# A perceiver layer's cross-attention: values of four batches weighed in one visit, sixteen probability buffers, context loads in pairs

## The chip, the cores and the metric

One core of a Trainium2 chip (trn2). The metric is the device time of the kernel in microseconds; a single execution is also recorded by the profiler. TensorE (PE) multiplies matrices, VectorE (DVE) and ScalarE (ACT) work on tiles in SBUF and PSUM, GpSimd (POOL) on tiles in SBUF, and SyncE (SP) issues the loads and stores. Every engine runs its own list of instructions in order and waits on semaphores that the others raise.

## What is computed

One layer over 128 batches of 32 tokens of 128 features: cross-attention to a context of 257 rows, then self-attention, then a mixture of experts. The change lies in the cross-attention, whose core in the reference is (16 heads of 8 features):

```
def _L0_xattn_ref(queries, keys, values, mask):
    q = queries.reshape(B, L, H, -1); k = keys.reshape(B, S, H, -1); v = values.reshape(B, S, H, -1)
    scores = jnp.einsum('blhe,bshe->bhls', q, k)
    A = jax.nn.softmax(scale * scores, axis=-1)
    A = A * mask
    out = jnp.einsum('bhls,bshd->blhd', A, v)
    ...
x = x + _L0_xattn_ref(_layernorm(x, axis=-1), ctx_1024, ctx_1024, fside_SxS2_0)
```

Here L is 32, S is 257, and keys and values are the same context. All of it is in float32.

## The kernel before

The 128 batches go in 16 tiles of eight (TB = 8). A tile has two halves of four batches (HB = 4) and 16 steps; the half of a step is its number divided by 8. A step takes two groups of heads, so two steps make a batch. The first and the last tile are written out, the 14 between run in a loop on every engine. In the text, step s means the step of that number in a half (0 to 7) or, above 7, in a tile (8 to 15).

*A step.* TensorE computes the scores of step s into one of two PSUM buffers SC (`scores`, L425). VectorE takes the row maxima (`maxima`, L613, instruction neg_max<-SC), ScalarE the exponentials and their sums (`exponentials`, L551, E<-SC). Two steps later TensorE turns these probabilities into a PSUM buffer ETP (`turn_probs`, L439, ETP<-ident,E), and VectorE multiplies them with the mask into a buffer of Et (`keep_probs`, L621). The scores of step s+2 wait for the exponentials of step s, which free the SC buffer. Each of the float32 score and value products stands as two instructions in the trace.

*A visit.* `weigh_values` (L450, AV<-Et,V) multiplies a batch's values, four groups of 32 columns, with its probabilities into the PSUM tile AV. TensorE's `lagging` calls it for two batches at a time, behind the scores and the turn of probabilities of steps 3, 7, 11 and 15. Et has eight buffers, one for each step of a half.

*Beside the steps.* TensorE's `steps` puts further work at fixed steps: after the scores of steps 0 and 8 `turn_queries` turns the normalised tokens xn (L404); in steps 2, 10, 6 and 14 `turn_keys` turns two batches of the context V into keys (L394), before the turn of probabilities in steps 2 and 10, behind it in steps 6 and 14; in steps 5 and 13 `turn_out` gathers the outputs (L462). All three go through one PSUM tile, MISC. The keys of steps 6 and 14 wait there until `own_outputs` has taken the outputs out (o_n). ScalarE copies keys (`keep_keys`, L533) and queries (`keep_queries`, L541) out of MISC; the scores of step 8 and of the next tile's step 0 wait for the keys turned in steps 6 and 14.

*VectorE's order* in a half: the maxima of a step, then the probabilities of two steps before. In between, at step 3, `invert`; at step 4, the token statistics (`norm_stats`, L580) ahead of the maxima and, behind them, the outputs out of AV (`keep_sums`, L640), `norm_mean`, the probabilities, `norm_var` and `last_probs`; at step 5, behind the probabilities, `own_outputs` (L652, O_n); at step 7, behind the probabilities, in the first half of a tile the transposition of O_n (`turn_tile`, L661), and then `normalise` (L600), which writes xn for the transpose that TensorE does in the next step.

*The loads* are on SyncE's queue, whose order is written out in its `steps`: x for the next tile, last context rows, and V (`load_ctx`, two batches, 256 KB) each behind a wait for the engine that frees its buffer. V has one buffer for each batch of a tile; the load of pair k waits until the visit that read the pair before is over (av_ps counts weighed batches).

Of the kernel before, what the change touches and what calls it, by code (L numbers as in the profile page):

```python
# [14 lines left out]
B, L, D = 128, 32, 128  # L15
# [7 lines left out]
P = 128  # L23
NQ, HQ = 4, 4
# [10 lines left out]
def perceiver_layer(nc, x, ctx, fmask, Wq, bq, Wk, bk, Wv, bv, Wo, bo, gate_w, w1, b1, w2, b2, ln_g, ln_b, out):  # L35
    with ExitStack() as es:
# [67 lines left out]
        with ExitStack() as s1:  # L104
            def sb1(name, shape, dt=F32):
                return s1.enter_context(nc.sbuf_tensor(name, shape, dt))
# [27 lines left out]
            E = sb1("E", [P, 2, HB * NQ, S])  # L134
            den = sb1("den", [P, 2, HB * NQ])
            rden = sb1("rden", [P, HB * NQ])
            Et = sb1("Et", [P, HSTEPS, 2, KT, HQ * L])
            O_m = sb1("O_m", [P, HB, HQ * L])
            O_n = sb1("O_n", [P, DK, TB * NQ])
            O_t = sb1("O_t", [P, DK, L])  # L140
# [52 lines left out]
            @block.sync  # L193
            def _(sp):
                def load_residual(q):

                    for b in range(TB):
                        sp.dma_start(X[32 * q + NQ * b:32 * q + NQ * b + NQ, :, :],
                                     x.rearrange("(t b) (g q e) c -> q b g t (e c)", t=T, g=NQ, q=HQ)[q, b]).then_inc(xperm_in, 16)

                def steps(t, fresh):

                    sp.wait_ge(xn_sb, 2 * t + 1)
                    sp.nop(nofuse=True)
                    load_x(sp, t + 1, 0)
                    sp.wait_ge(qt_ps, 2 * t + 1)
                    sp.nop(nofuse=True)
                    load_last(sp, t + 1, 0)
                    if not fresh:
                        sp.wait_ge(av_ps, TB * t)  # L210
                        sp.nop(nofuse=True)
                        load_ctx(sp, t, 3)
                        sp.wait_ge(o_last, 2 * t)
                        sp.nop(nofuse=True)
                        load_all(sp, t, 1)
                    if fresh:
                        for q in range(HQ // 2):
                            load_residual(q)
                    sp.wait_ge(av_ps, TB * t + 2)
                    sp.nop(nofuse=True)  # L220
                    load_ctx(sp, t + 1, 0)
                    sp.wait_ge(xn_sb, 2 * t + 2)
                    sp.nop(nofuse=True)
                    load_x(sp, t + 1, 1)
                    sp.wait_ge(qt_ps, 2 * t + 2)
                    sp.nop(nofuse=True)
                    load_last(sp, t + 1, 1)
                    sp.wait_ge(av_ps, TB * t + 4)
                    sp.nop(nofuse=True)
                    load_ctx(sp, t + 1, 1)  # L230
                    sp.wait_ge(o_last, 2 * t + 1)
                    sp.nop(nofuse=True)
                    load_all(sp, t + 1, 0)
                    if fresh:
                        for q in range(HQ // 2, HQ):
                            load_residual(q)
                    sp.wait_ge(av_ps, TB * t + 6)
                    sp.nop(nofuse=True)
                    load_ctx(sp, t + 1, 2)

                sp.dma_start(fm[:, :], fmask).then_inc(setup_in, 16)
                load_x(sp, 0, 0)
                load_last(sp, 0, 0)
                load_ctx(sp, 0, 0)
                for n, src in zip("qkvo", (Wq, Wk, Wv, Wo)):
                    sp.dma_start(W[n][:, :], src).then_inc(w2_in, 16)
                for i, src in enumerate((bq, bk, bv)):
                    sp.dma_start(brow[i:i + 1, :], src.unsqueeze(0)).then_inc(w2_in, 16)
                sp.dma_start(bo_row[:, :], bo.unsqueeze(0)).then_inc(w2_in, 16)
                sp.dma_start(b1_rows[:, :], b1.rearrange("e (a f) -> (e a) f", a=FH)).then_inc(b1_in, 16)  # L250
                load_x(sp, 0, 1)
                load_ctx(sp, 0, 1)
                load_last(sp, 0, 1)
                load_ctx(sp, 0, 2)
                load_ctx(sp, 0, 3)
                load_all(sp, 0, 0)
                load_all(sp, 0, 1)
                steps(0, True)
                with sp.Fori(1, T - 1) as t:
                    steps(t, False)  # L260
                sp.wait_ge(av_ps, TB * (T - 1))
                load_ctx(sp, T - 1, 3)
                sp.wait_ge(o_last, 2 * (T - 1))
                load_all(sp, T - 1, 1)

                sp.dma_start(W1[:, :, :], w1.rearrange("e c f -> c e f")).then_inc(w3_in, 16)
                sp.dma_start(G[:, :], gate_w).then_inc(w3_in, 16)
                for a in range(FH):
                    sp.dma_start(W2[:, :, a, :], w2[:, a * P:(a + 1) * P, :].rearrange("e f d -> f e d")).then_inc(w3_in, 16)
                sp.dma_start(b2r[:, :, :].rearrange("p e d -> p (e d)"),  # L270
                             b2.rearrange("e d -> (e d)").unsqueeze(0).to_broadcast([P, NE * D])).then_inc(w3_in, 16)
                sp.dma_start(gr[:, :, :].rearrange("p e d -> p (e d)"),
                             ln_g.rearrange("e d -> (e d)").unsqueeze(0).to_broadcast([P, NE * D])).then_inc(w3_in, 16)
                sp.dma_start(b_rows[:, :], ln_b).then_inc(w3_in, 16)
# [98 lines left out]
            def _(pe):  # L373
# [68 lines left out]
                def weigh_values(t, j, first=False):  # L442

                    h = j // HB
                    pe.wait_ge(et_sb, STEPS * t + 2 * j + 2)
                    if j % HB == 0 and not first:
                        pe.wait_ge(o_m, 2 * t + h)
                    for k in range(KT):
                        for g in range(NQ):
                            i = pe.matmul(AV[32 * g:32 * g + 32, j % HB, :], V[:, j, k, 32 * g:32 * g + 32],  # L450
                                          Et[:, 2 * (j % HB) + g // 2, g % 2, k, :],
                                          start=(j % HB == 0 and k == 0), stop=(j % HB == HB - 1 and k == KT - 1),
                                          skip_group_check=True)
                    i.then_inc(av_ps, 1)
# [11 lines left out]
                def back(t, s, lag):  # L466

                    return (t, s - lag) if s >= lag else (t - 1, s + STEPS - lag)

                def lagging(t, s):  # L470

                    fresh = isinstance(t, int) and t == 0
                    if not (fresh and s < 2):
                        tt, ss = back(t, s, 2)
                        turn_probs(tt, ss, first=fresh and s < 4)
                    if s % 4 == 3 and not (fresh and s < HSTEPS - 1):
                        tt, ss = back(t, s, 2 + 5)
                        weigh_values(tt, ss // 2, first=fresh and s < HSTEPS)
                        weigh_values(tt, ss // 2 + 1)
                    if s % HSTEPS == 5 and not (fresh and s < HSTEPS):  # L480
                        tt, ss = back(t, s, HSTEPS)
                        turn_out(tt, ss // HSTEPS)
# [39 lines left out]
                run_tiles(steps, pe)  # L522
                turn_probs(T - 1, STEPS - 2)
                turn_probs(T - 1, STEPS - 1)
                weigh_values(T - 1, TB - 2)
                weigh_values(T - 1, TB - 1)
                turn_out(T - 1, 1, final=True)

            @block.scalar
# [47 lines left out]
            def _(dve):  # L577
# [37 lines left out]
                def keep_probs(t, s, first=False):  # L615

                    n = STEPS * t + s
                    dve.wait_ge(et_ps, n + 1)
                    if not first:
                        dve.wait_ge(av_ps, TB * t + s // 2 - 3)  # L620
                    dve.tensor_tensor(Et[:, s % HSTEPS, :, :, :].rearrange("p u k c -> p (u k c)"), ETP[s % 2][:, :],  # L621
                                      mask_T[:, :, :, :].rearrange("p u k c -> p (u k c)"), ALU.mult).then_inc(et_sb, 1)

                def invert(t, h):
# [41 lines left out]
                def steps(t, fresh, final):  # L666
                    for s in range(STEPS):
# [6 lines left out]
                            norm_mean(t + 1, s // HSTEPS)  # L674
                        if not (fresh and s < 2):
                            tt, ss = back(t, s, 2)
                            keep_probs(tt, ss, first=fresh and s < HSTEPS + 2)
# [1028 lines left out]
```

## Time and profile before

| | us |
|---|---|
| median of 3 runs | 1048.88 (1048.84 to 1049.33) |
| the profiled execution | 1050.45 |
| its span in the profile | 1048.7 |
| busy: TensorE matmul / weight load | 927.9 / 815.4 |
| busy: VectorE / ScalarE / GpSimd | 840.0 / 648.9 / 606.9 |

The cross-attention is the first half of the span: its first visit starts at 36.4 us and its last ends near 525 us; self-attention and the experts follow. The mean granted clock of TensorE is 0.965 of 2.4 GHz over the span. The rows shown further below are of three kinds: sums over a stretch (windows), sums over a line, and single entries of the timeline, each with its start, its duration, the engine, the line and the tile that is written and read; a bracket at the end gives idle time before it and what ended that. A duration may overlap the next one's start on the same engine, since the engines are pipelined; the distance between two starts is what one of them cost.

### The profile page before, as it was taken

To read this page: it belongs to the slowest core of one execution; us is meant where nothing else is said; L and a number is where in the kernel's file an instruction comes from. 1 tells how busy PE (TensorE), PEld (TensorE's weight loads), DVE (VectorE), ACT (ScalarE), POOL (GpSimd) and SP (SyncE) were. 2 spreads that over 40 slices of the span, in tenths; PEclk is the share of its full clock that TensorE was granted. 3 is DMA by queue.
4 is the path that set the end of the run, shared out by engine and by line. 5 is a ranking of instruction groups with operands and counts; after the bars stand their busy time and mean duration, and the time that the engine had idled before them with its cause. 6 is when DMAs were issued, how large, how long until landed. Compare 5 with 4: busy or idle time off the path is not lost. (4 is left out here: it accounts for less than half of the span.)

```text
span 1048.7 us, 25999 instructions
## 1 busy us (share of the span) xinstructions
PE 927.9 (88%) x7666; PEld 815.4 (78%) x7666; DVE 840.0 (80%) x2152; ACT 648.9 (62%) x2006; POOL 606.9 (58%) x531
## 2 busy tenths in 40 slices
PE   3959999999999999999948888878899888888983
PEld 2848888888888888888848888778788787878872
DVE  5747787878788787878758887886499999999995
ACT  2626566656666566666536666666477777767674
POOL 4335555655555564556344444443477777877786
PEclk9979999999999999999969998999999999999997
DMA  4021212212221212221400000000000000000000
GB/s 119 25 74 56 58 50 65 55 47 60 55 65 43 65 55 52 56 65 54 142 1 1 0 0 0 0 0 1 1 2 10 5 10 5 10 5 6 9 5 16
DMA packets 48676, 35.34 MB, mean 34 GB/s; under 512 B 3660, under 2 KB 48392, under 8 KB 48648
## 3 DMA queue, kind: packets, MB, share of 16 engines
q1 hardware_dynamic: 48648, 35.00, 12.2%
q8 instruction: 14, 0.23, 0.1%
q14 instruction: 14, 0.11, 0.0%
HBM read 32.88 MB, written 2.10 MB: 33 GB/s over the span
## 5 line engine op out<-in xcount | busy, mean ns | idle before, releaser
L551 ACT ACTIVATE E<-SC,neg_max 128x257 f32<-128x257 f32 x512 | 238.4, 471 | 161.2 <-DVE neg_max L613 161.1
L425 PE MATMUL SC<-Kt,Qbd 128*128 128x257 f32 x1024 | 279.6, 396 | 1.0 <-ACT E L551 0.8
L613 DVE TENSOR_REDUCE neg_max<-SC 128x2 f32<-128x514 f32 x256 | 177.0, 691 | 86.6 <-PE SC L425 75.2
L425 PEld LDWEIGHTS SC<-Kt,Qbd 128*128 128x128 f32 x1024 | 176.9, 193 | 31.4 <-issue 14.1
L301 POOL TENSOR_TENSOR Qbd<-Qt,head_scaled 128x2048 f32<-128x2048 f32 (+2 forms) x33 | 145.1, 4398 | 80.0 <-ACT Qt L541 80.0
L621 DVE TENSOR_TENSOR Et<-ETP,mask_T 128x512 f32<-128x512 f32 x256 | 174.0, 680 | 15.0 <-PE ETP L439 14.9
L439 PE MATMUL ETP<-ident,E 128*128 128x128 f32 x1024 | 156.1, 275 | 0.0
L1371 PE MATMUL PO<-W,hid 128*128 128x128 f32 x1024 | 138.2, 278 | 18.8 <-ACT hid L1412 18.7
L1371 PEld LDWEIGHTS PO<-W,hid 128*128 128x128 f32 x1024 | 131.4, 192 | 29.0 <-issue 21.5
L1436 ACT ACTIVATE Y<-Z,zb,zs 128x128 f32<-128x128 f32 x256 | 111.0, 485 | 60.1 <-DVE zb L1591 60.1
L439 PEld LDWEIGHTS ETP<-ident,E 128*128 128x128 f32 x1024 | 125.3, 142 | 20.5 <-issue 0.4
L1360 PE MATMUL PH<-xT,W 128*128 128x256 f32 x512 | 135.1, 387 | 0.5 <-ACT xT L1404 0.5
L1412 ACT ACTIVATE hid<-PH,b1c 128x256 f32<-128x256 f32 x256 | 105.5, 463 | 19.3 <-PE PH L1360 17.8
L551 ACT ACTIVATION_READ_ACCUMULATOR E<-SC,neg_max 128x1 f32 x512 | 101.1, 198 | 0.0
L308 POOL TENSOR_TENSOR xrs<-xvar,neg_half 128x1 f32<-128x1 f32 x32 | 17.6, 549 | 134.8 <-DVE xvar L593 134.8
L1360 PEld LDWEIGHTS PH<-xT,W 128*128 128x128 f32 x512 | 87.8, 192 | 9.7 <-ACT xT L1404 0.7
L1268 POOL TENSOR_TENSOR zr<-zv,neg_half 128x8 f32<-128x8 f32 x32 | 60.0, 1875 | 39.6 <-DVE zv L1577 39.6
L1262 POOL TENSOR_TENSOR XB<-xn,b2r 128x512 f32<-128x512 f32 x64 | 81.4, 1275 | 0.8 <-DVE xn L1487 0.8
L1601 DVE TENSOR_TENSOR U<-Y,gr 128x512 f32<-128x512 f32 x64 | 71.2, 1113 | 5.4 <-POOL acc L1274 2.9
L450 PE MATMUL AV<-Et,V 128*32 128x128 f32 x2048 | 69.4, 276 | 0.3 <-DVE Et L621 0.3
L1120 PE MATMUL PY<-Wo,Oc 128*128 128x128 f32 x256 | 39.1, 316 | 29.5 <-DVE Oc L887 29.5
L450 PEld LDWEIGHTS AV<-Et,V 128*32 128x32 f32 x2048 | 51.9, 109 | 11.4 <-issue 10.7
(161 smaller groups left out, 1579.1 us busy)
## 6 DMA issues: line engine op xcount, KB each, us to landing
V<-in_ctx_dram SPq DMA_DIRECT2D x64, 256.0 KB, 2.9
last_all<-in_ctx_dram SPq DMA_DIRECT2D x32, 256.0 KB, 5.0
xh<-in_x_dram SPq DMA_DIRECT2D x32, 64.0 KB, 3.7
X<-in_x_dram SPq DMA_DIRECT2D x32, 64.0 KB
out_dram<-Xo SPq DMA_DIRECT2D x64, 32.0 KB, 1.5
W<-in_L_ffn_w_dram SPq DMA_DIRECT2D x1, 1024.0 KB
W<-in_L_ffn_w_dram SPq DMA_DIRECT2D x2, 512.0 KB
last_row<-in_ctx_dram SPq DMA_DIRECT2D x32, 2.0 KB
```

The source lines that it names most:

```text
L301: pool.tensor_tensor(Qbd[:, h, j0:j1, :, :], Qt[:, j0:j1, :].unsqueeze(2).to_broadcast([P, j1 - j0, H, L]), head_scaled[:, :, :].unsqueeze ...
L425: i = pe.matmul(SC[s % 2][:, u, 0:S], Qbd[:, h, jj, g:g + HQ, :].rearrange("p q l -> p (q l)"), Kt[:, h, jj, 0:S], start=True, stop=True)
L439: i = pe.transpose(ETP[s % 2][:, c:c + P], E[:, h, u0 + u, k * P:(k + 1) * P], ident[:, :])
L450: i = pe.matmul(AV[32 * g:32 * g + 32, j % HB, :], V[:, j, k, 32 * g:32 * g + 32], Et[:, 2 * (j % HB) + g // 2, g % 2, k, :], start=(j % H ...
L551: i = act.activation(E[:, h, u0 + u, :], SC[s % 2][:, u, 0:S], ACT.Exp, bias=neg_max[:, s % 2, u:u + 1], accum_out=den[:, h, u0 + u:u0 + u ...
L613: dve.tensor_reduce(neg_max[:, s % 2, :], SC[s % 2][:, :, 0:S], AX.X, ALU.max, negate=True).then_inc(max_sb, 1)
L621: dve.tensor_tensor(Et[:, s % HSTEPS, :, :, :].rearrange("p u k c -> p (u k c)"), ETP[s % 2][:, :], mask_T[:, :, :, :].rearrange("p u k c ...
L1262: pool.tensor_tensor(XB[:, 2 * p:2 * p + 2, :, :], xn[:, :, :].unsqueeze(1).to_broadcast([P, 2, 2, D]), b2r[:, 2 * p:2 * p + 2, :].unsquee ...
L1360: i = pe.matmul(PH[x % 2][:, a, :], W1[:, x, a * P:(a + 1) * P], xT[:, :], start=True, stop=True)
L1371: i = pe.matmul(PO[p % 2][:, 2 * (x % 2) + e, :], hid[:, x % 2, a, e * P:(e + 1) * P], W2[:, x, a, :], start=(a == 0), stop=(a == FH - 1))
L1412: i = act.activation(hid[:, x % 2, a, :], PH[x % 2][:, a, :], ACT.Gelu, bias=b1c[:, FH * x + a:FH * x + a + 1])
L1436: i = act.activation(Y[:, p % 2, k, :], Z[:, p, k, :], ACT.Identity, scale=zs[:, p // 2, f:f + 1], bias=zb[:, p // 2, f:f + 1])
```

## The change

TensorE weighs the four batches of a half in one visit, in steps 2 and 10 (behind the scores, the turn of keys and the turn of probabilities), in place of two visits of two batches. The visit in step 10 takes the first half of the same tile, that in step 2 the second half of the tile before. Et has 16 buffers, one for each step of a tile, and `keep_probs` waits for the visit that read the buffer one tile before. The loads of V go in pairs behind the two visits: pairs 2 and 3 of a tile behind step 2, pairs 0 and 1 of the next tile behind step 10. Behind the last tile four batches are weighed in place of two.

```
--- before.py
+++ after.py
@@ -134,7 +134,7 @@
             E = sb1("E", [P, 2, HB * NQ, S])
             den = sb1("den", [P, 2, HB * NQ])
             rden = sb1("rden", [P, HB * NQ])
-            Et = sb1("Et", [P, HSTEPS, 2, KT, HQ * L])
+            Et = sb1("Et", [P, STEPS, 2, KT, HQ * L])
             O_m = sb1("O_m", [P, HB, HQ * L])
             O_n = sb1("O_n", [P, DK, TB * NQ])
             O_t = sb1("O_t", [P, DK, L])
@@ -209,6 +209,7 @@
                     if not fresh:
                         sp.wait_ge(av_ps, TB * t)
                         sp.nop(nofuse=True)
+                        load_ctx(sp, t, 2)
                         load_ctx(sp, t, 3)
                         sp.wait_ge(o_last, 2 * t)
                         sp.nop(nofuse=True)
@@ -216,9 +217,6 @@
                     if fresh:
                         for q in range(HQ // 2):
                             load_residual(q)
-                    sp.wait_ge(av_ps, TB * t + 2)
-                    sp.nop(nofuse=True)
-                    load_ctx(sp, t + 1, 0)
                     sp.wait_ge(xn_sb, 2 * t + 2)
                     sp.nop(nofuse=True)
                     load_x(sp, t + 1, 1)
@@ -227,6 +225,7 @@
                     load_last(sp, t + 1, 1)
                     sp.wait_ge(av_ps, TB * t + 4)
                     sp.nop(nofuse=True)
+                    load_ctx(sp, t + 1, 0)
                     load_ctx(sp, t + 1, 1)
                     sp.wait_ge(o_last, 2 * t + 1)
                     sp.nop(nofuse=True)
@@ -234,10 +233,6 @@
                     if fresh:
                         for q in range(HQ // 2, HQ):
                             load_residual(q)
-                    sp.wait_ge(av_ps, TB * t + 6)
-                    sp.nop(nofuse=True)
-                    load_ctx(sp, t + 1, 2)
-
                 sp.dma_start(fm[:, :], fmask).then_inc(setup_in, 16)
                 load_x(sp, 0, 0)
                 load_last(sp, 0, 0)
@@ -259,6 +254,7 @@
                 with sp.Fori(1, T - 1) as t:
                     steps(t, False)
                 sp.wait_ge(av_ps, TB * (T - 1))
+                load_ctx(sp, T - 1, 2)
                 load_ctx(sp, T - 1, 3)
                 sp.wait_ge(o_last, 2 * (T - 1))
                 load_all(sp, T - 1, 1)
@@ -448,7 +444,7 @@
                     for k in range(KT):
                         for g in range(NQ):
                             i = pe.matmul(AV[32 * g:32 * g + 32, j % HB, :], V[:, j, k, 32 * g:32 * g + 32],
-                                          Et[:, 2 * (j % HB) + g // 2, g % 2, k, :],
+                                          Et[:, 2 * j + g // 2, g % 2, k, :],
                                           start=(j % HB == 0 and k == 0), stop=(j % HB == HB - 1 and k == KT - 1),
                                           skip_group_check=True)
                     i.then_inc(av_ps, 1)
@@ -473,10 +469,10 @@
                     if not (fresh and s < 2):
                         tt, ss = back(t, s, 2)
                         turn_probs(tt, ss, first=fresh and s < 4)
-                    if s % 4 == 3 and not (fresh and s < HSTEPS - 1):
-                        tt, ss = back(t, s, 2 + 5)
-                        weigh_values(tt, ss // 2, first=fresh and s < HSTEPS)
-                        weigh_values(tt, ss // 2 + 1)
+                    if s % HSTEPS == 2 and not (fresh and s < HSTEPS):
+                        tt, ss = back(t, s, HSTEPS + 2)
+                        for j in range(HB):
+                            weigh_values(tt, ss // 2 + j, first=fresh)
                     if s % HSTEPS == 5 and not (fresh and s < HSTEPS):
                         tt, ss = back(t, s, HSTEPS)
                         turn_out(tt, ss // HSTEPS)
@@ -522,8 +518,8 @@
                 run_tiles(steps, pe)
                 turn_probs(T - 1, STEPS - 2)
                 turn_probs(T - 1, STEPS - 1)
-                weigh_values(T - 1, TB - 2)
-                weigh_values(T - 1, TB - 1)
+                for j in range(HB, TB):
+                    weigh_values(T - 1, j)
                 turn_out(T - 1, 1, final=True)
 
             @block.scalar
@@ -617,8 +613,8 @@
                     n = STEPS * t + s
                     dve.wait_ge(et_ps, n + 1)
                     if not first:
-                        dve.wait_ge(av_ps, TB * t + s // 2 - 3)
-                    dve.tensor_tensor(Et[:, s % HSTEPS, :, :, :].rearrange("p u k c -> p (u k c)"), ETP[s % 2][:, :],
+                        dve.wait_ge(av_ps, TB * t + HB if s >= STEPS - 2 else TB * (t - 1) + HB * (s // HSTEPS + 1))
+                    dve.tensor_tensor(Et[:, s, :, :, :].rearrange("p u k c -> p (u k c)"), ETP[s % 2][:, :],
                                       mask_T[:, :, :, :].rearrange("p u k c -> p (u k c)"), ALU.mult).then_inc(et_sb, 1)
 
                 def invert(t, h):
@@ -674,7 +670,7 @@
                             norm_mean(t + 1, s // HSTEPS)
                         if not (fresh and s < 2):
                             tt, ss = back(t, s, 2)
-                            keep_probs(tt, ss, first=fresh and s < HSTEPS + 2)
+                            keep_probs(tt, ss, first=fresh or (isinstance(tt, int) and tt == 0))
                         if s % HSTEPS == 0 and not (final and s >= HSTEPS):
                             place_last(*((t, 1) if s < HSTEPS else (t + 1, 0)))
                         if not final and s % HSTEPS == 4:
```

## Rows read from the trace of the kernel before

**Rows 1.** Windows of two whole tiles: busy us and instructions of each engine, clock, DMA.

```profile
core 0: us, PE busy (x) PEld busy (x) DVE busy (x) ACT busy (x) POOL busy (x), PEclk, DMA share, GB/s
204.80:235.16 30.36, 30.36 (x293) 25.67 (x292) 24.46 (x51) 18.85 (x70) 17.26 (x15) 1.00 0.21 56
235.16:265.53 30.37, 30.37 (x293) 25.68 (x292) 24.48 (x51) 18.85 (x70) 17.25 (x15) 1.00 0.20 56
```

**Rows 2.** Timeline of TensorE, tiles around 200 to 220 us: start, duration, work.

```profile
201.45 1.03 PE L425 MATMUL SC<-Kt,Qbd 128*128 128x257 f32 x4
...
202.85 1.08 PE L450 MATMUL AV<-Et,V 128*32 128x128 f32 x32
203.86 1.13 PE L425 MATMUL SC<-Kt,Qbd 128*128 128x257 f32 x4
204.83 0.27 PE L404 MATMUL MISC<-ident,xn 128*128 128x128 f32 x1
...
205.67 1.03 PE L425 MATMUL SC<-Kt,Qbd 128*128 128x257 f32 x4
...
206.98 1.03 PE L425 MATMUL SC<-Kt,Qbd 128*128 128x257 f32 x4
...
211.13 1.13 PE L425 MATMUL SC<-Kt,Qbd 128*128 128x257 f32 x4
...
212.54 1.03 PE L425 MATMUL SC<-Kt,Qbd 128*128 128x257 f32 x4
...
216.04 0.63 PE L394 MATMUL MISC<-ident,V 128*128 128x128 f32 x4
216.51 1.03 PE L425 MATMUL SC<-Kt,Qbd 128*128 128x257 f32 x4
...
219.90 0.27 PE L404 MATMUL MISC<-ident,xn 128*128 128x128 f32 x1
```

**Rows 3.** Groups by line, cross-attention: the weighing of the values.

```profile
L450 PE MATMUL AV<-Et,V 128*32 128x128 f32 x2048 | 69.4, 276 | 0.3 <-DVE Et L621 0.3
```

**Rows 4.** Timeline of VectorE behind a visit, steps 3 to 5.

```profile
209.79 0.69 DVE L613 TENSOR_REDUCE neg_max<-SC 128x2 f32<-128x514 f32 x1
...
211.16 0.23 DVE L580 BATCH_NORM_STATS2 xstat<-xh 128x6 f32<-128x128 f32 x1
...
212.30 0.69 DVE L613 TENSOR_REDUCE neg_max<-SC 128x2 f32<-128x514 f32 x1 [0.91 <-PE SC L425]
...
214.39 0.68 DVE L613 TENSOR_REDUCE neg_max<-SC 128x2 f32<-128x514 f32 x1
...
215.59 0.38 DVE L652 TENSOR_TENSOR O_n<-MISC,rden 128x128 f32<-128x128 f32 x1
```

**Rows 5.** Timeline of VectorE, step 7 of both halves of a tile.

```profile
202.52 0.69 DVE L613 TENSOR_REDUCE neg_max<-SC 128x2 f32<-128x514 f32 x1 [0.54 <-PE SC L425]
...
203.13 0.68 DVE L621 TENSOR_TENSOR Et<-ETP,mask_T 128x512 f32<-128x512 f32 x1
...
203.73 0.43 DVE L661 STREAM_TRANSPOSE O_t<-O_n 128x256 f32<-128x256 f32 x1
...
204.08 0.30 DVE L600 TENSOR_SCALAR xn<-xh,xmv,xrs 128x128 f32<-128x128 f32 x1
...
217.58 0.69 DVE L613 TENSOR_REDUCE neg_max<-SC 128x2 f32<-128x514 f32 x1 [0.48 <-ACT E L551]
...
218.79 0.34 DVE L600 TENSOR_SCALAR xn<-xh,xmv,xrs 128x128 f32<-128x128 f32 x1
```

**Rows 6.** Timeline of ScalarE: its copy of the keys of step 6.

```profile
217.45 0.59 ACT L533 ACTIVATE Kt<-MISC 128x512 f32<-128x512 f32 x1
```

**Rows 7.** Timeline of TensorE, last tile: scores of its steps 8 and 10.

```profile
507.38 1.13 PE L425 MATMUL SC<-Kt,Qbd 128*128 128x257 f32 x4
...
510.35 1.14 PE L425 MATMUL SC<-Kt,Qbd 128*128 128x257 f32 x4
```

**Rows 8.** The loads of V by their line: time to landing.

```profile
DMA to landing us min/median/max: 2.6/2.9/7.8
```

More of the change, by code:

```diff
@@ L136, in perceiver_layer @@
             rden = sb1("rden", [P, HB * NQ])
-            Et = sb1("Et", [P, HSTEPS, 2, KT, HQ * L])
+            Et = sb1("Et", [P, STEPS, 2, KT, HQ * L])
             O_m = sb1("O_m", [P, HB, HQ * L])
@@ L211, in steps @@
                         sp.nop(nofuse=True)
+                        load_ctx(sp, t, 2)
                         load_ctx(sp, t, 3)
@@ L218, in steps @@
                             load_residual(q)
-                    sp.wait_ge(av_ps, TB * t + 2)
-                    sp.nop(nofuse=True)
-                    load_ctx(sp, t + 1, 0)
                     sp.wait_ge(xn_sb, 2 * t + 2)
@@ L229, in steps @@
                     sp.nop(nofuse=True)
+                    load_ctx(sp, t + 1, 0)
                     load_ctx(sp, t + 1, 1)
@@ L236, in steps @@
                             load_residual(q)
-                    sp.wait_ge(av_ps, TB * t + 6)
-                    sp.nop(nofuse=True)
-                    load_ctx(sp, t + 1, 2)
                 sp.dma_start(fm[:, :], fmask).then_inc(setup_in, 16)
@@ L261, in _ @@
                 sp.wait_ge(av_ps, TB * (T - 1))
+                load_ctx(sp, T - 1, 2)
                 load_ctx(sp, T - 1, 3)
@@ L450, in weigh_values @@
                             i = pe.matmul(AV[32 * g:32 * g + 32, j % HB, :], V[:, j, k, 32 * g:32 * g + 32],
-                                          Et[:, 2 * (j % HB) + g // 2, g % 2, k, :],
+                                          Et[:, 2 * j + g // 2, g % 2, k, :],
                                           start=(j % HB == 0 and k == 0), stop=(j % HB == HB - 1 and k == KT - 1),
@@ L475, in lagging @@
                         turn_probs(tt, ss, first=fresh and s < 4)
[L476 to L479, printed above, removed]
+                    if s % HSTEPS == 2 and not (fresh and s < HSTEPS):
+                        tt, ss = back(t, s, HSTEPS + 2)
+                        for j in range(HB):
+                            weigh_values(tt, ss // 2 + j, first=fresh)
                     if s % HSTEPS == 5 and not (fresh and s < HSTEPS):
@@ L524, in _ @@
                 turn_probs(T - 1, STEPS - 1)
-                weigh_values(T - 1, TB - 2)
-                weigh_values(T - 1, TB - 1)
+                for j in range(HB, TB):
+                    weigh_values(T - 1, j)
                 turn_out(T - 1, 1, final=True)
@@ L619, in keep_probs @@
                     if not first:
-                        dve.wait_ge(av_ps, TB * t + s // 2 - 3)
-                    dve.tensor_tensor(Et[:, s % HSTEPS, :, :, :].rearrange("p u k c -> p (u k c)"), ETP[s % 2][:, :],
+                        dve.wait_ge(av_ps, TB * t + HB if s >= STEPS - 2 else TB * (t - 1) + HB * (s // HSTEPS + 1))
+                    dve.tensor_tensor(Et[:, s, :, :, :].rearrange("p u k c -> p (u k c)"), ETP[s % 2][:, :],
                                       mask_T[:, :, :, :].rearrange("p u k c -> p (u k c)"), ALU.mult).then_inc(et_sb, 1)
@@ L676, in steps @@
                             tt, ss = back(t, s, 2)
-                            keep_probs(tt, ss, first=fresh and s < HSTEPS + 2)
+                            keep_probs(tt, ss, first=fresh or (isinstance(tt, int) and tt == 0))
                         if s % HSTEPS == 0 and not (final and s >= HSTEPS):
```

## The prediction

> **What bounds the kernel now.** I read the windows first. Over two whole tiles of the cross-attention stage TensorE is busy for 30.36 of 30.36 us and 30.37 of 30.37 us, at full granted clock (1.00, 2.4 GHz), while VectorE, the next, has 24.46 and 24.48 us [rows 1]. So a tile costs what TensorE's ordered list of work costs, plus any wait in it. The timeline of TensorE then shows what a step is worth. A plain step (scores, then a turn of probabilities) takes 206.98 - 205.67 = 1.31 us from one score to the next. A step with a visit of two batches takes 203.86 - 201.45 = 2.41 us, and the plain step after a visit 212.54 - 211.13 = 1.41 us [rows 2]. A visit of two therefore costs 1.10 + 0.10 = 1.20 us.
>
> Last I looked at what is *nearly* late. VectorE's queue is in order, and the normalised tokens xn come at the end of its step 7, behind the maxima of step 7, the probabilities of step 5 and, in one half of each tile, the transposition of O_n. Their end, 204.38 and 219.13 us [rows 5], stands against the transpose of xn on TensorE, which begins at 204.83 and 219.90 us [rows 2]. The cover is 0.45 and 0.77 us. What makes it is the visit at the end of step 7, which this change moves away.
>
> **The change part by part.** I measure T in us from the score of step 3, the first one after the new visit.
>
> *One visit in place of two (a gain).* The 32 matmuls of a visit last 1.08 us in all, a single one 0.276 us on average [rows 2, 3]; so 31 starts take 0.80 us, 26 ns each, and 32 stream in 0.83 us. The other 1.20 - 0.83 = 0.37 us is paid on entering and leaving. A visit of four costs 1.20 + 0.83 = 2.03 us, against 2.40 us: a gain of 0.37 us a half, 0.74 us a tile. Bounds: nothing, if the entry price grew with the number of matmuls, and 0.37 us. I take the upper end, since the matmuls inside a visit run evenly, with no gap between its two batches.
>
> *After the visit, step 5 waits (a loss).* Steps 3 and 4 are both plain now, 1.41 + 1.31 = 2.72 us. But the score of step 5 needs the scores buffer of step 3, which must pass maxima and exponentials. The last tile, which turns no queries at its step 8, shows that loop bare behind a visit: from 507.38 to 510.35 us is 2.97 us [rows 7]. So the score of step 5 is at T = 2.97, a stall of 0.25 us. Bounds: nothing, and 0.5 us if the loop is also late by VectorE's extra work.
>
> *VectorE's steps 3 to 7.* The maxima of step 3 start at T = 1.17 (212.30 - 211.13 after a visit). From there to the end of the token statistics VectorE is continuous: 209.79 to 211.16 + 0.23, which is 1.60 us; so the maxima of step 4 are at T = 2.77. From those to the maxima of step 5 it is continuous again, 214.39 - 212.30 = 2.09 us: T = 4.86. From there to the score of step 7 I read 216.51 - 214.39 = 2.12 us, through the outputs O_n, which the turn of keys in step 6 waits for: T = 6.98 [rows 2, 4]. By TensorE's own list steps 5 and 6 take 216.51 - 212.54 = 3.97 us today, which from 2.97 gives 6.94: the two ways agree within 0.04 us. The short wait for O_n is there today as well: O_n ends at 215.97 and the keys follow at 216.04.
>
> *The tokens of step 7 (the main loss).* The maxima of step 7 start 217.58 - 216.51 = 1.07 us behind its score, at T = 8.05. From their start to the end of xn it is 219.13 - 217.58 = 1.55 us without the transposition and 204.38 - 202.52 = 1.86 us with it [rows 5]. So xn is ready at 9.60 or 9.91. TensorE has only a plain step (1.31) and a score (0.97 - 0.10 = 0.87) in front of the transpose of xn, and would be there at 6.98 + 2.18 = 9.16. The hand-over from VectorE takes about 0.1 us (O_n's end to the keys, 0.07). The transpose comes at 9.70 or 10.01: a stall of 0.54 or 0.85 us, where there was none. This is the removed cover: 1.20 us go from in front of it, 0.45 to 0.77 us were slack. Bounds: 0.3 to 1.0 us a half. ScalarE's copy of step 6's keys, which the score of step 8 needs, ends 217.45 + 0.59 - 216.51 = 1.53 us behind the score of step 7 [rows 6], at 8.51; TensorE would be ready for that score at 8.29. This delay lies inside the same stall, because the transpose behind that score waits longer still, so I add nothing.
>
> *The rest of the half.* From the transpose of xn to the next score 205.67 - 204.83 = 0.84 us, a plain step 1.31 us, then step 2 with its turn of keys (0.47, from 216.04 to 216.51) and the visit of four (1.10 + 0.83): 1.31 + 0.47 + 1.93 = 3.71 us. The half is 9.70 + 0.84 + 1.31 + 3.71 = 15.56 us, or 15.87 us with the transposition; a tile 31.43 us.
>
> *Sixteen buffers.* A buffer is written again eight steps after the visit that read it (steps 2 and 10 of a tile): VectorE's new wait is met long before, and I cost it at nothing. Inside the new visit the fourth batch needs the probabilities of step 7, turned in step 9; in front of it on TensorE stand the score of step 10, a turn of keys, a turn of probabilities and three batches (3 x 0.42 us), about 3 us in all, against 0.68 us for VectorE's product: no wait there.
>
> *The loads.* The SyncE queue passes its two wait points on the contexts with two loads at each. The load of x for the second half and its last row go ahead of the burst, and their own waits are met by then. The first of a pair must land before the turn of keys of step 6, at T = 6.5, and leaves just after the visit, near T = 0.3: 6.2 us. A load lands in 2.6 to 7.8 us, 2.9 in the median [rows 8]; two on top of each other, 5.8 us by doubling the median. I cost it at nothing, with the cover of steps 3 to 6.
>
> **The sum.** 31.43 - 30.37 = +1.06 us a tile. Between the first and the last of the new visits stand 15 tiles (30 halves): +15.9 us. The edges (first half, tail behind the last tile) change by less than 1 us, and I leave them out. The profiled execution took 1050.45 us with a span of 1048.7 us; 1066.4 us is the sum on it. The runs' median, 1048.88, is 1.57 us lower than that execution: **1064.8 us**, 1.5% slower.
>
> **The rivals.**
> *A, forecast.* The waits of steps 5 and 8 take more than the visits give back. For it: the cover is 0.45 and 0.77 us and 1.20 us go. 0.84.
> *B, TensorE stays dense.* Then only the gain counts: 30 x 0.37 = 11 us less, 1037.8 us. The point that decides is the score of step 8: if xn ended within 0.87 us of that score's start, nothing would wait. For it speak the busy windows with no gap; against it, that xn is chained to the score of step 7 by 1.07 + 1.55 us on an in-order queue, with 2.18 us of TensorE's work beside it. Beside this stands a rule of the Trainium skill, Perfetto Trace Analysis, section Identifying the Most-Contended Engine: work is to be taken off the engine with the highest occupancy first. By that rule taking work from TensorE would pay in full, as in B. The rows bear it out only as far as they show TensorE the busiest; the chain through VectorE is not in an occupancy. 0.08.
> *C, the burst comes late.* If a pair took 7.8 us, the largest landing seen, the keys of step 6 would come 1.6 us late in every half: up to 48 us on top of A, near 1110 us. It decides from a landing of 6.2 us on. Against it: 2.9 us in the median. 0.04.
> *D, gain and waits cancel*: stalls at the lower bounds, 0.3 and 0.5 us at step 8 and 0.1 us at step 5, and 0.2 us of today's small waits gone, give 1.0 - 0.74 - 0.2, +0.1 us a tile: 1050 us. 0.04.
> That the change doesn't do what it says cannot be: the loop weighs four batches in one place.
>
> **How the numbers follow.** 0.2% is 2.1 us, about what a measurement here can tell from no change. The range follows from the bounds inside A. Low: stalls of 0.4, 0.6 and twice 0.1 us less 0.74 and 0.2, +0.3 us a tile, 1053 us. High: stalls of 0.7 and 1.0 us, twice 0.4 us, half the gain, +2.1 us a tile, 1081 us, a corner of all three; I close at 1078. Outside lie B, C, most of D and some tail of A, together under 0.2. Faster 0.09 (B and a little), same 0.05, slower 0.86.
>
> **What the new profile would show.** Visits of 64 matmuls of about 1.9 us, two a tile; the transpose of xn 0.1 us behind the end of xn, and 1.1 to 1.7 us behind the score of step 8 in place of 0.97; the score of step 5 about 2.97 us behind that of step 3; a tile of 31.4 us. TensorE's busy time in such a window would no longer fill it. The prediction is wrong if xn ends before TensorE comes for it, or if the keys of step 6 wait for a load of V.

## The result and the profile after

The changed kernel takes 1073.36 us in the median of 4 runs (1072.58 to 1076.49) against 1049.08 us, so 24.3 us slower; the ratio of the means is 1.0237, 95% interval 1.0215 to 1.0259. The forecast was 1064.8 us (1053 to 1078): the sign and the mechanism held, the size was too small. The profiled execution has a span of 1072.4 us, 23.7 us more than before. Of these 23.3 us stand at the end of the cross-attention: its last gathering of outputs starts at 548.82 us, before at 525.53.

The windows of two tiles of the changed kernel, cut where a half's visit is over (columns as in [rows 1]):

```profile
200.40:232.43 32.03, 30.84 (x297) 25.88 (x293) 24.49 (x51) 18.73 (x70) 17.25 (x15) 1.00 0.18 53
232.43:264.49 32.06, 30.84 (x296) 25.88 (x292) 24.48 (x51) 18.73 (x70) 17.28 (x15) 1.00 0.19 53
```

A tile takes 32.03 and 32.06 us, in place of 30.36 and 30.37 [rows 1]: 1.68 us more, 25 us over 15 tiles. TensorE is busy for 30.84 us of it and idle for 1.2 us, where it was idle for none before; VectorE has the 24.48 us it had. The time is in waits of TensorE. The idle time shows only a part of them: TensorE's busy time grew by 0.48 us although its list of work got shorter; a score that was held, for one, shows 1.13 us in place of 1.03. Its timeline, first the half with the transposition of O_n, then the one without (compare [rows 2]):

```profile
200.40 1.13 PE L421 MATMUL SC<-Kt,Qbd 128*128 128x257 f32 x4
...
203.37 1.13 PE L421 MATMUL SC<-Kt,Qbd 128*128 128x257 f32 x4
...
207.41 1.03 PE L421 MATMUL SC<-Kt,Qbd 128*128 128x257 f32 x4
...
209.11 1.13 PE L421 MATMUL SC<-Kt,Qbd 128*128 128x257 f32 x4 [0.23 <-ACT Kt L529]
210.58 0.32 PE L400 MATMUL MISC<-ident,xn 128*128 128x128 f32 x1 [0.35 <-DVE xn L596]
...
212.78 1.03 PE L421 MATMUL SC<-Kt,Qbd 128*128 128x257 f32 x4
...
214.62 1.95 PE L446 MATMUL AV<-Et,V 128*32 128x128 f32 x64
216.50 1.13 PE L421 MATMUL SC<-Kt,Qbd 128*128 128x257 f32 x4
...
225.42 1.13 PE L421 MATMUL SC<-Kt,Qbd 128*128 128x257 f32 x4 [0.43 <-ACT Kt L529]
226.38 0.31 PE L400 MATMUL MISC<-ident,xn 128*128 128x128 f32 x1
...
228.61 1.13 PE L421 MATMUL SC<-Kt,Qbd 128*128 128x257 f32 x4
...
232.43 1.14 PE L421 MATMUL SC<-Kt,Qbd 128*128 128x257 f32 x4
```

Count from the score of step 3 at 200.40. The score of step 5 comes at 2.97 us and that of step 7 at 7.01; the score of step 8 stands at 8.71, the transpose of xn at 10.18, the visit begins at 14.22 and the next half at 16.10. The other half lasts 15.93 us (216.50 to 232.43), with the score of step 8 at 8.92 and the transpose at 9.88. What ends the waits stands in the brackets and in the table of waits from 40 to 540 us (engine and line, what it waited for: us in total, times, longest):

```profile
PEld SC L421 <- ACT E L547: 10.9, 33, 0.3
...
PE SC L421 <- ACT Kt L529: 9.0, 27, 0.5
PE MISC L400 <- DVE xn L596: 5.6, 14, 0.9
```

In the same stretch of the kernel before, the exponentials ended 0.5 us of such waits in all, and the other two none. ScalarE's copy of the keys (L529, 27 times) and VectorE's xn (L596, 14 times, one half in two) are the two at step 8. The exponentials (L547) are the wait of step 5. The rows of VectorE and ScalarE that released them (compare [rows 5, 6]):

```profile
208.38 0.59 ACT L529 ACTIVATE Kt<-MISC 128x512 f32<-128x512 f32 x1
208.48 0.69 DVE L609 TENSOR_REDUCE neg_max<-SC 128x2 f32<-128x514 f32 x1 [0.45 <-PE SC L421]
...
210.05 0.31 DVE L596 TENSOR_SCALAR xn<-xh,xmv,xrs 128x128 f32<-128x128 f32 x1
...
224.49 0.60 ACT L529 ACTIVATE Kt<-MISC 128x512 f32<-128x512 f32 x1
...
225.80 0.34 DVE L596 TENSOR_SCALAR xn<-xh,xmv,xrs 128x128 f32<-128x128 f32 x1
```

In the first half xn ends at 210.36 and the transpose follows at 210.58. In the second xn ends at 226.14, but there the score at 225.42 had itself waited for the keys, which end at 225.09, and the transpose comes 0.96 us behind that score. The two waits end almost together there: 226.14 and the 0.22 us of the first half would give 226.36, against 226.38.

### The profile page after: what moved, and what is told of

Read it like the earlier page. It is cut to its first block and busy times, and to the rows that moved or that the text cites. A ratio compares the mean times of both kernels' runs of the same rounds, so it can differ in the third digit from the quotient of the medians.

```text
span 1072.4 us, 25977 instructions
## 1 busy us (share of the span) xinstructions
PE 935.1 (87%) x7666; PEld 818.2 (76%) x7666; DVE 839.4 (78%) x2152; ACT 647.1 (60%) x2006; POOL 606.9 (57%) x531
## 5 line engine op out<-in xcount | busy, mean ns | idle before, releaser
L547 ACT ACTIVATE E<-SC,neg_max 128x257 f32<-128x257 f32 x512 | 238.2, 471 | 196.6 <-DVE neg_max L609 196.3
L547 ACT ACTIVATION_READ_ACCUMULATOR E<-SC,neg_max 128x1 f32 x512 | 101.1, 197 | 0.0
L446 PE MATMUL AV<-Et,V 128*32 128x128 f32 x2048 | 62.5, 274 | 0.0
L1116 PEld LDWEIGHTS PY<-Wo,Oc 128*128 128x128 f32 x256 | 37.0, 230 | 32.5 <-DVE Oc L883 32.5
```

What stands on the lines that cost most here:

```text
L547: i = act.activation(E[:, h, u0 + u, :], SC[s % 2][:, u, 0:S], ACT.Exp, bias=neg_max[:, s % 2, u:u + 1], accum_out=den[:, h, u0 + u:u0 + u ...
L1116: i = pe.matmul(PY[:, e * D:(e + 1) * D], Oc[:, a:a + HQ, :, :].rearrange("p a b g -> p (a b g)"), W["o"][:, :], start=(q == 0), stop=(q = ...
```

## The experiments

Each ratio is to the kernel before on the same chip; that kernel's median was 1050 to 1054 us on these chips. Runs are compared with each other by these ratios.

**Which part of the change costs.** The visits of two put back, buffers and paired loads kept:

```
-                    if s % HSTEPS == 2 and not (fresh and s < HSTEPS):
...
+                    if s % 4 == 3 and not (fresh and s < HSTEPS - 1):
+                        tt, ss = back(t, s, 2 + 5)
+                        weigh_values(tt, ss // 2, first=fresh and s < HSTEPS)
+                        weigh_values(tt, ss // 2 + 1)
```

> The changed kernel with the visits put back to two batches behind steps 3, 7, 11 and 15, but with its sixteen buffers and its loads of V in pairs kept (now behind the visits of steps 3 and 11). Theory (the moved visit took the cover from the tokens and the keys of step 7): the whole loss is the visits', so this runs as the kernel before, 1049 us within 2 us. Rival (the pairs of loads or the buffers cost time): it stays well above, towards 1073 us, and the keys of step 6 or 14 wait for a load of V.

Measured: 1051.26 us, ratio 0.9996 (0.9979 to 1.0012). The buffers and the pairs of loads cost nothing that 0.2% would show; a load of V landed in 2.9 us in the median, 6.3 at most. Then the same number of visits as before the change, moved but not merged:

```
+                    if s % HSTEPS in (2, 3) and not (fresh and s < HSTEPS):
+                        tt, ss = back(t, s, HSTEPS + s % HSTEPS)
+                        for j in range(2 * (s % HSTEPS) - 4, 2 * (s % HSTEPS) - 2):
+                            weigh_values(tt, ss // 2 + j, first=fresh)
```

> The changed kernel with the four batches of a half weighed in two visits of two, behind steps 2 and 3 (10 and 11): as many visits as before the change, but none at step 7. Theory (the loss comes from taking the visit away from step 7, not from making it long): the waits of step 8 stay; the score of step 5 is covered again, an entry price of 0.33 us a half comes back. A half is 16.1 us with the transposition and 15.8 us without, a tile 31.95 us: 24 us above the kernel before, within 4 us, near 1073 us. Rival (one long visit of 64 matmuls costs the time by itself): near the kernel before, 1049 to 1055 us.

Measured: 1073.48 us, ratio 1.0202 (1.0175 to 1.0228). It is the place of the visits that costs, not their length; and in this place the merging gives nothing back, since the changed kernel has 1.0237. The wait is the same one; TensorE's timeline of this run at step 8:

```profile
203.19 1.13 PE L421 MATMUL SC<-Kt,Qbd 128*128 128x257 f32 x4
...
211.80 0.32 PE L400 MATMUL MISC<-ident,xn 128*128 128x128 f32 x1 [0.43 <-DVE xn L596]
...
219.36 1.13 PE L421 MATMUL SC<-Kt,Qbd 128*128 128x257 f32 x4
...
235.26 0.92 PE L421 MATMUL SC<-Kt,Qbd 128*128 128x257 f32 x3
```

The halves are 16.17 and 15.90 us, 32.07 us a tile (31.95 expected).

**Whether step 8 is where it waits.** VectorE's tokens one step earlier, one condition changed:

```
-                        if not final and s % HSTEPS == 7:
+                        if not final and s % HSTEPS == 6:
                             normalise(t + 1, s // HSTEPS)
```

> The changed kernel with VectorE's normalisation of the tokens moved from its step 7 to its step 6; nothing else. Theory: in the half with the transposition of O_n the transpose of xn no longer waits for xn but for the score of step 8, 0.5 us earlier (10.18 to 9.68 us behind the score of step 3); in the other half the score of step 8, which waits for ScalarE's keys, already sets it, so little changes there. 15 tiles by 0.5 us: 1066 us. Rival (the wait for xn is only beside a longer one): 1073 us unchanged. Rival (xn is the whole loss): back to 1049 us.

Measured: 1066.95 us, ratio 1.0148 (1.0109 to 1.0186), 0.9% under the changed kernel. Timeline of TensorE, the half with the transposition and then the one without:

```profile
198.38 1.14 PE L421 MATMUL SC<-Kt,Qbd 128*128 128x257 f32 x4
...
207.09 1.13 PE L421 MATMUL SC<-Kt,Qbd 128*128 128x257 f32 x4 [0.23 <-ACT Kt L529]
208.05 0.27 PE L400 MATMUL MISC<-ident,xn 128*128 128x128 f32 x1
...
213.93 1.13 PE L421 MATMUL SC<-Kt,Qbd 128*128 128x257 f32 x4
...
222.84 1.13 PE L421 MATMUL SC<-Kt,Qbd 128*128 128x257 f32 x4 [0.43 <-ACT Kt L529]
...
229.85 1.13 PE L421 MATMUL SC<-Kt,Qbd 128*128 128x257 f32 x4
```

The half without the transposition is 229.85 - 213.93 = 15.92 us, as it was (15.93): there ScalarE's keys still hold the score of step 8 (222.84, 8.91 us behind 213.93). The transpose of xn now follows that score by 0.96 to 0.97 us in both halves; the gain is all in the other half, 15.55 us in place of 16.10. Next, work put into the waits:

```
                         lagging(t, s)
+                        if s % HSTEPS == 7:
+                            pe.wait_ge(o_m, 2 * t + s // HSTEPS)
+                            for r in range(8):
+                                pe.transpose(AV[:, r % HB, :], ident[:, :], ident[:, :])
```

> The changed kernel with eight transposes of the identity into the idle AV tile added behind step 7 of each half on TensorE, 8 x 0.109 = 0.87 us of work a half that nothing reads. Theory (TensorE stands idle there, for VectorE's xn and ScalarE's keys): the work goes into the stalls, nothing in the half with the transposition and about 0.2 us in the other, so 0 to 4 us in all: 1073 to 1078 us. Rival (TensorE's list is the bound and its work costs in full): 31 halves by 0.87 us, 1100 us.

Measured: 1080.24 us, ratio 1.0268 (1.0225 to 1.031), 0.3% over the changed kernel, which is inside the intervals of the two; the full price would be 2.5%. Timeline of TensorE:

```profile
199.96 1.13 PE L421 MATMUL SC<-Kt,Qbd 128*128 128x257 f32 x4
...
208.28 1.04 PE L493 MATMUL AV<-ident 128*128 128x128 f32 x8
209.15 1.03 PE L421 MATMUL SC<-Kt,Qbd 128*128 128x257 f32 x4
210.14 0.33 PE L400 MATMUL MISC<-ident,xn 128*128 128x128 f32 x1
...
232.18 1.13 PE L421 MATMUL SC<-Kt,Qbd 128*128 128x257 f32 x4
```

The filler ends and the score follows at 209.15; the transpose of xn stands at 10.18 us behind 199.96, where it was without the filler. A tile is 32.22 us, 0.18 more, for 1.74 us of added work.

**What is left when both chains are shorter.** Tokens in step 6 and, besides:

```
+                        if s % HSTEPS == 5 and not (fresh and s < HSTEPS):
+                            tt, ss = back(t, s, HSTEPS)
+                            own_outputs(tt, ss // HSTEPS)
                         if not (fresh and s < 2):
...
                         if s == 6:
                             turn_keys(t, 2)
...
+                        lagging(t, s)
...
-                        if s == 7:
+                        if s == 6:
                             keep_keys(t, 2)
```

> The changed kernel with both chains of step 7 shortened: the tokens normalised in step 6; the outputs O_n taken before the probabilities of step 5; the keys of steps 6 and 14 turned before the probabilities; ScalarE's copy of these keys put before the exponentials of step 6. Theory: the score of step 8 stands at 8.3 us and the transpose of xn at 9.2 us behind the score of step 3, a half is about 15.1 us, a tile 30.2 us, against 32.04 us of the changed kernel: 1046 us, a little faster than the kernel before, with the wait of step 5 (0.25 us) as the only one left. Rival (the loop from scores over maxima and exponentials binds all plain steps, 2.87 us for two): the half stays over 15.4 us and the kernel at 1055 us or more.

Measured: 1057.33 us, ratio 1.0067 (1.0052 to 1.0082): the step-8 waits are gone, but the half is 15.37 us, not 15.1. The forecast of 1046 us was missed, and the rival (over 15.4 us, 1055 us or more) was nearly right. Two successive visits in the timeline, and the wait that is left:

```profile
208.69 1.96 PE L446 MATMUL AV<-Et,V 128*32 128x128 f32 x64
...
224.06 1.96 PE L446 MATMUL AV<-Et,V 128*32 128x128 f32 x64
```

```profile
PEld SC L421 <- ACT E L547: 12.6, 46, 0.3
```

So I spread TensorE's small works over the stretch without visits, one for every two steps: queries in steps 4 and 12, odd pairs of keys in steps 0 and 8, with the copies, the last row, the tokens and the transposition moved to suit (waits adjusted):

```
-                        if s == 0:
+                        if s == 4:
                             turn_queries(t, 1)
...
-                        if s % HSTEPS == 2:
+                        if s % HSTEPS == 0:
                             turn_keys(t, 1 + 2 * (s // HSTEPS))
...
-                            if s == 7:
-                                turn_tile(tt)
+                        if s == 10 and not fresh:
+                            turn_tile(t - 1)
```

> The kernel of the run before with tokens and keys early, visits of four, with TensorE's small works spread so that no two plain steps follow each other far from the visit: the queries turned in steps 4 and 12, the keys of the odd pairs in steps 0 and 8, their copies on ScalarE before the exponentials of steps 1 and 9, the last context row placed in step 4, the tokens normalised in step 7 again, O_n transposed in step 10. Theory (what is left in that kernel is the loop from a score over maxima and exponentials to the score two steps on, 2.87 us against 2.62 us of two plain steps, in steps 5 and 10): both waits go, about 0.17 us stays at step 8 for ScalarE's copy of the keys, a half is 15.0 us, a tile 30.0 us: 4 to 6 us under the kernel before, 1044 us. Rival (VectorE's own order in steps 3 to 6 binds, wherever TensorE's works stand): a half over 15.2 us and no gain on the kernel before.

> The same order of small works, with visits of two behind steps 3, 7, 11 and 15 as in the kernel before. Theory: every entry price of a visit is paid (0.33 us a half more than with visits of four), and the visit of step 7 covers the copy of the keys: a half is 15.1 to 15.2 us, 1046 to 1049 us, 2 to 4 us over the run with visits of four. Rival (the spread order alone is what gains, visits of four earn nothing): as the run with visits of four, or below it.

Measured: 1164.97 us, ratio 1.1073 (1.1048 to 1.1099), and 1146.9 us, 1.0907 (1.0883 to 1.093), with visits of two. Both theories, which had 1044 and 1046 to 1049 us, missed a new wait. The timeline of GpSimd, VectorE and TensorE in the first of the two shows it, with a window of TensorE half a tile earlier (columns as in [rows 1]):

```profile
224.35 4.49 POOL L297 TENSOR_TENSOR Qbd<-Qt,head_scaled 128x2048 f32<-128x2048 f32 x1 [10.94 <-ACT Qt L538]
...
225.19 0.68 DVE L618 TENSOR_TENSOR Et<-ETP,mask_T 128x512 f32<-128x512 f32 x1
...
225.85 3.03 DVE L630 SCALAR_TENSOR_TENSOR last_p<-E,mask_col,rden 128x16 f32<-128x16 f32 x1
...
229.91 1.09 PE L387 MATMUL MISC<-ident,V 128*128 128x128 f32 x4 [2.38 <-DVE O_n L649]
```

```profile
209.50:215.50 6.00, 6.00 (x20) 5.08 (x21) 3.38 (x6) 3.24 (x13) 3.45 (x6) 0.50 0.08 22
```

VectorE's small product last_p (128 x 16) began at 225.85 and lasted 3.03 us, until GpSimd's Qbd ended (224.35 + 4.49 = 228.84). TensorE then waited 2.38 us for O_n, and about as long once in every half. Behind the same wait of the half before, 2.28 us, its granted clock was 0.50, the lower of its two levels (1.2 GHz), for the 6 us of the window; over the two halves from 221.18 to 258.90 us it was 0.91. In the next pair last_p stands ahead of Qbd:

```
                                 invert(tt, hh)
-                            if s % HSTEPS == 4:
                                 last_probs(tt, hh)
```

> The run with the small works spread and visits of four, with one change: VectorE's last_p product (two inputs in SBUF) moved from step 4, where GpSimd's 4.5 us product Qbd now runs beside it, to step 3, ahead of it. Theory (in the run with the works spread, last_p waited for Qbd to end, 3.03 us in place of 0.23, and the 1165 us come from that alone): last_p takes 0.23 us again, the half is 15.0 us, and the kernel comes to 4 to 6 us under the kernel before, 1044 us. Rival (last_p is long for another reason, as its wait for GpSimd's last_o): it stays at 3 us in step 3, or the kernel stays above 1100 us.

> The same move of last_p with visits of two behind steps 3, 7, 11 and 15. Theory: a half of 15.1 to 15.2 us, each visit's entry price paid twice, 2 to 4 us slower than with visits of four, 1046 to 1049 us. Rival (visits of four earn nothing even when nothing is late): the same time as with visits of four, or less.

Measured: 1054.25 us, ratio 1.0015 (1.0003 to 1.0028), and 1058.83 us, 1.0062 (1.0041 to 1.0082), with visits of two. The durations of last_p by its line (min/median/max ns), first in the spread run, then here:

```profile
L630 DVE SCALAR_TENSOR_TENSOR last_p<-E,mask_col,rden x32: 230/3028/3336, 45.7 to 636.5; 128x16 f32<-128x16 f32 x32
```

```profile
L630 DVE SCALAR_TENSOR_TENSOR last_p<-E,mask_col,rden x32: 241/243/247, 42.6 to 525.4; 128x16 f32<-128x16 f32 x32
```

The 111 us between these runs come from the place of that one product, with the clock that fell with it. But the expected gain on the kernel before was missed, and so was the time with visits of two. The timeline of VectorE and TensorE with visits of four shows a cause:

```profile
228.45 0.69 DVE L637 TENSOR_TENSOR O_m<-AV,hh_of 128x512 f32<-128x512 f32 x1
...
228.75 0.60 PE L432 MATMUL ETP<-ident,E 128*128 128x128 f32 x4
...
229.14 0.14 DVE L603 COPY Kt<-MISC 128x4 f32<-128x4 f32 x1
...
229.42 1.05 PE L459 MATMUL MISC<-gather_d,O_m 128*128 128x32 f32 x8
```

The gathering of the outputs (L459) starts 0.67 us behind the turn of probabilities before it, in place of the 0.44 us that four transposes take: it waits for VectorE, which takes the sums out of AV until 229.14 and places the last row (L603) until 229.28. The remedy tried is VectorE's idle time during a long visit:

```
-                            if s % HSTEPS == 3:
+                            if s % HSTEPS == 2:
                                 invert(tt, hh)
                                 last_probs(tt, hh)
...
+                        if s == 2 and not fresh:
+                            normalise(t, 1)
+                        if s == 10 and not final:
+                            normalise(t + 1, 0)
```

with `place_last` ahead of `keep_sums` in step 4.

> The run with the small works spread, visits of four and last_p ahead of Qbd, whose half is 15.2 to 15.35 us, with VectorE's small works moved to where TensorE's long visit leaves it idle: the reciprocal, last_p and the normalisation of the tokens in step 2 (10), behind the probabilities, and the last context row placed ahead of the sums of step 4. Theory (what is left there are VectorE's late starts: the gathering of outputs waits 0.15 to 0.24 us for the last row, the exponentials of step 8 start 0.4 us late behind the tokens): the gathering stands at 4.43 us, the score of step 8 at 8.4 and the visit's end at 14.9 us behind the score of step 3; a tile 29.8 us, 6 to 9 us under the kernel before. Rival (the loop of scores, maxima and exponentials or the restart of 0.1 us behind every wait binds): a half over 15.1 us, within 0.2% of the kernel before.

Measured: 1043.48 us (1041.48 to 1046.55), ratio 0.9911 (0.9891 to 0.9932): 0.9% faster than the kernel before and about 3% faster than the changed one, as expected. Four works moved at once, so the run doesn't say what each of them is worth. The scores behind three visits in its timeline, halves of 14.97 and 14.82 us:

```profile
206.30 1.13 PE L418 MATMUL SC<-Kt,Qbd 128*128 128x257 f32 x4
...
221.27 1.13 PE L418 MATMUL SC<-Kt,Qbd 128*128 128x257 f32 x4
...
236.09 1.13 PE L418 MATMUL SC<-Kt,Qbd 128*128 128x257 f32 x4
```

The last run asks what the long visits are worth in that order:

> The fastest run's order of all works, with visits of two behind steps 3, 7, 11 and 15 in place of visits of four. Theory (a visit's entry price of 0.33 to 0.37 us is paid once more in every half, and nothing else changes on TensorE's list): a tile 30.4 to 30.5 us, 10 us over the run with visits of four, within 3 us of the kernel before. Rival (the new order alone gave the 9 us, the long visits nothing): the time of the run with visits of four, 0.99 of the kernel before.

Measured: 1058.59 us, ratio 1.0067 (1.0043 to 1.0091). Timeline of TensorE:

```profile
205.99 1.13 PE L418 MATMUL SC<-Kt,Qbd 128*128 128x257 f32 x4
...
207.83 1.03 PE L418 MATMUL SC<-Kt,Qbd 128*128 128x257 f32 x4
...
210.70 1.14 PE L418 MATMUL SC<-Kt,Qbd 128*128 128x257 f32 x4
...
221.40 1.13 PE L418 MATMUL SC<-Kt,Qbd 128*128 128x257 f32 x4
```

That is 8 us over the kernel before, where 3 at most were expected. The half is 15.41 us, 0.52 more than with visits of four. Entering and leaving twice is 0.33 of it, by twice 1.20 less the 2.07 us measured for a visit of four. The rest is a wait in the loop from a score over its maxima and exponentials to the score two steps on: 207.83 to 210.70 is 2.87 us for two plain steps that otherwise take 2.62. The two make 0.58; why 0.06 us of that do not show was not traced. So the new order is slower than the old one with visits of two, and faster with visits of four: order and visits go together.

## Why the prediction was right

*TensorE bound, cover lost at step 7: right.* The chains of steps 3 to 7 came where the sum put them: the score of step 5 at 2.97 (2.97 forecast), of step 7 at 7.01 (6.98), the maxima of step 7 at 8.08 (8.05), the end of xn at 9.96 (9.91), all in the half with the transposition. The transpose stands 1.47 us behind the score of step 8 there, inside the 1.1 to 1.7 us named as a sign, and 0.96 us in the other half, where the score itself was late. The runs that move the visits without merging, move the tokens, and fill the idle time show it as the cause.

*The gain of a visit: nearly right.* A visit of four costs (216.50 - 212.78) less a plain step of 1.31 and the turn of keys of 0.44, and 0.10 behind it: 2.07 us, against twice 1.20. The gain is 0.33 us a half, forecast 0.37.

*The terms that were too small: from xn to the next visit.* With the transposition the half is 16.10 us (15.87 forecast), without it 15.93 (15.56). In the first, the hand-over from xn to its transpose (from the end of the one to the start of the other) was taken as 0.1 us and measured 0.22 (210.36 to 210.58); that is half of the difference, and the rest is in pieces of 0.05 and 0.06 us.

In the second, half of the 0.37 us stands at the transpose, at 9.88 in place of 9.70. The step "I add nothing" for ScalarE's keys failed here: they ended at 8.59 (8.51 forecast), but the score of step 8 came at 8.92 and held the transpose. From the keys to that score it is 0.33 us, against 0.14 in the other half (208.97 to 209.11). The later score is the first work of a new round of TensorE's loop; whether that is the reason was not tried. The other half of the 0.37 us lies behind the transpose and was there in the kernel before. The prediction took that stretch from the rows of one half for both: the score of step 10 follows the transpose by 2.23 us (226.38 to 228.61) in place of 2.15 and takes 1.13 us in place of 1.03, as this row did before, with its transpose at 219.90 [rows 2]:

```profile
222.13 1.13 PE L425 MATMUL SC<-Kt,Qbd 128*128 128x257 f32 x4
```

All this is 0.60 us a tile and 9 us over 15 tiles. With the forecast's 15.9 us it makes 25, and the edges gave a little back of it. The stalls in front of the transpose, against the 9.16 us of TensorE's own list, were 1.02 and 0.72 us, where 0.85 and 0.54 were forecast and 1.0 was the upper bound. So the mechanism was foreseen; that the time lies in the range is due to the width that the range gave to these stalls, and not to the sum.

*The rivals.* B (TensorE dense, 1037.8 us) fell on the spot it named: in the half with the transposition xn ended 1.25 us behind the start of the score of step 8, and not within 0.87. In the other half it ended 0.72 us behind it, but only because the keys had held that score, at 8.92 in place of the 8.29 us of TensorE's own list. The rule of the Trainium skill beside it (Perfetto Trace Analysis, Identifying the Most-Contended Engine) says to optimize the most-contended engine first, and judges TensorE by MFU, which no run here gives, or by the busy share of its weight loads. The trace agrees that TensorE is that engine: its weight loads have 25.67 of 30.36 us, VectorE 24.46 [rows 1]. That less work on it is less time is not what the page states; the prediction drew it as rival B, and it did not come out: TensorE's busy time fell short of the window by 1.2 us a tile. C (late pairs) is excluded by the run with visits of two and paired loads, and by the changed kernel itself, where a load of V landed in 2.8 us in the median, 6.2 at most, and no wait of TensorE ends with one. D fell with the measured stalls.

## What to carry to other kernels

Before work is taken out of a full engine's list, ask which late arrivals it was hiding: here 1.2 us of visit stood in front of tokens that had 0.45 and 0.77 us to spare. In this case the saving on the busiest engine was paid out only when the chains that ran beside the removed work were moved too: the edit alone cost 2.4%, with the new order it came out 0.9% under the kernel before, and the new order alone was 0.7% over it. And a small work that is moved has to be looked at beside what the other engines do at its new time.

## What the runs showed of the hardware that was not expected

A VectorE product with both inputs in SBUF (last_p) took 3.03 us in place of 0.23 beside a 4.5 us GpSimd product and ended with it, at 228.88 and 228.84 us; a VectorE product with an input in PSUM (Et<-ETP,mask_T, at 225.19) took 0.68 us beside the same GpSimd product. The GPSIMD Engine Reference of the Trainium skill, section Specifications, says that GpSimd shares its SBUF interfaces with VectorE and contends with VectorE instructions that have two SBUF inputs. The trace agrees, and shows the product held until GpSimd's instruction had ended.

A score whose start was held by a wait takes 1.13 us in place of 1.03, and its successor comes 0.96 to 0.97 us behind it in place of 0.87; this 0.10 us, which I had put down to the end of a visit, is paid behind waits too, as at 203.37 and 225.42. Why this is so was not tried.
